# Two scores at once on the two halves of TensorE's rows, heads stacked at partitions 0 and 64, in a fused attention and expert kernel

## What is computed

```python
qkv = (x @ qkv_w.T + qkv_b).reshape(B, T, 3, H, dh)
scores = jnp.einsum('bhtd,bhsd->bhts', q, k) * scale          # dh ** -0.5
scores = jnp.where(causal, -jnp.inf, scores)
attn = jax.nn.softmax(scores, axis=-1)
seq_out = jnp.einsum('bhts,bhsd->bhtd', attn, v)
...
x = _layernorm(x + (seq_out + gated * mem_val) @ out_w.T + out_b)
x = _layernorm(x + mixture(x))   # top 2 of 8 true and 2 null experts
```

## Time and profile before

| what | value |
|---|---|
| median of 3 runs | 829.73 us (829.0 to 835.29) |
| the profiled execution's own time | 834.11 us |
| its span, first to last instruction | 832.4 us |
| mean granted TensorE clock | 0.946 |
| busy: PE, VectorE, ACT, GpSimd | 88%, 73%, 42%, 51% of the span |

### The profile page before, as it was taken

The page is one execution under the profiler, slowest core; times in us unless marked ns, Lnnn a source line. Parts: engine busy times, 40 slices in busy tenths (PEclk is TensorE's granted clock), DMA queues, the critical chain, the costliest instruction groups (busy, mean ns, idle before and its releaser), DMA issues.

```text
span 832.4 us, 12395 instructions
## 1 busy us (share of the span) xinstructions
PE 734.4 (88%) x4004; PEld 495.0 (59%) x4004; DVE 603.8 (73%) x2105; ACT 351.0 (42%) x701; POOL 422.3 (51%) x334
## 2 busy tenths in 40 slices
PE   6993998898898998999898998878899899998995
PEld 3452655565565666565565664446677676776774
DVE  2344776778878888889688877736777877787785
ACT  2211555446454545555455555842242242232410
POOL 9200894996665676668476893424134042240410
PEclk9995999999998999999899997899999999999998
DMA  7899589675564574655734747220220302303000
GB/s 274 257 234 165 127 142 144 163 115 104 130 102 84 133 119 100 152 85 138 139 69 105 139 87 170 73 101 2 77 85 18 101 10 93 102 1 102 26 24 27
DMA packets 60420, 89.88 MB, mean 108 GB/s; under 512 B 8234, under 2 KB 37316, under 8 KB 60356
## 3 DMA queue, kind: packets, MB, share of 16 engines
q1 hardware_dynamic: 60356, 89.09, 47.7%
HBM read 54.72 MB, written 33.82 MB: 106 GB/s over the span
## 4 chain that ended last, share of the span: by engine, by line
PE 47%; DVE 23%; DMA 10%; POOL 9%; ACT 4%; issue 4%; SPq 2%; ACTq 0%; POOLq 0%; DVEq 0%
PE ps L1256 15%; PE ps L374 8%; PE ps L338 7%; PE ps L327 6%; PE ps L315 6%; DVE ps L468 5%; DMA Wm<-mem_scratch 3%; DVE Ob L516 3%; DMA Q<-MT 3%; DVE A L1390 3%; ACT X L1242 2%; PE ps L1221 2%; PE ps L232 1%; POOL Pr L612 1%; DVE Z L1276 1%
## 5 line engine op out<-in xcount | busy, mean ns | idle before, releaser
L468 DVE CUSTOM_DVE_ANT_0 ps<-ps,mask 128x256 f32<-128x256 f32 (+3 forms) x512 | 236.9, 509 | 31.8 <-PE ps L315 31.0
L411 ACT ACTIVATE Pr<-ps 128x512 f32<-128x512 f32 (+2 forms) x384 | 190.1, 528 | 114.8 <-PE ps L327 110.6
L327 PE MATMUL ps<-Q,K 98*128 98x256 f32 (+2 forms) x512 | 173.2, 380 | 28.9 <-DMA Q<-MT 21.9
L315 PE MATMUL ps<-K,Q 96*128 96x256 f32 (+2 forms) x512 | 157.9, 355 | 23.2 <-DVE nmax L468 22.5
L1256 PE MATMUL ps<-ew_hi,XT 128*128 128x512 f32 x512 | 176.2, 403 | 0.0
L1390 DVE SCALAR_TENSOR_TENSOR A<-ps,cw,A 128x256 f32<-128x256 f32 x256 | 123.6, 483 | 48.5 <-PE ps L1256 36.0
L327 PEld LDWEIGHTS ps<-Q,K 98*128 98x128 f32 x512 | 94.1, 197 | 104.8 <-ACT Pr L411 61.0
L612 POOL TENSOR_SCALAR_AFFINE_SELECT Pr<-Pr 128x512 f32<-128x512 f32 x128 | 88.3, 704 | 103.2 <-ACT Pr L411 100.8
L315 PEld LDWEIGHTS ps<-K,Q 96*128 96x128 f32 x512 | 103.0, 203 | 45.8 <-DVE nmax L468 28.3
L1256 PEld LDWEIGHTS ps<-ew_hi,XT 128*128 128x128 f32 x512 | 97.0, 189 | 21.2 <-issue 0.3
L1256 PE MATMUL ps<-ew_rest,XT 128*128 128x512 f32 x256 | 101.2, 395 | 0.0
(11 more groups left out here) (190 smaller groups left out, 1049.2 us busy)
## 6 DMA issues: line engine op xcount, KB each, us to landing
qk_scratch<-HL SPq DMA_DIRECT2D x32, 512.0 KB, 3.2
Q<-qk_scratch SPq DMA_DIRECT2D x96, 128.0 KB, 4.4
K<-qk_scratch SPq DMA_DIRECT2D x96, 128.0 KB, 5.7
Pr<-xT SPq DMA_DIRECT2D x8, 512.0 KB, 7.0
xraw<-xT SPq DMA_DIRECT2D x8, 512.0 KB, 6.4
mem_scratch<-Rl SPq DMA_DIRECT2D x16, 256.0 KB, 7.5
mv_scratch<-MV SPq DMA_DIRECT2D x32, 128.0 KB, 1.8
Wm<-mem_scratch SPq DMA_DIRECT2D x16, 256.0 KB, 9.3
```

The source lines that it names most:

```text
L315: last = nc.tensor.matmul(o, Q[0:STACK, hh, P * i:P * i + P], K[0:STACK, hh, 0:n], start=True, stop=True)
L327: last = nc.tensor.matmul(o, K[0:STACK + 2, hh, P * kt:P * kt + P], Q[0:STACK + 2, hh, T - n:T], start=True, stop=True)
L411: nc.scalar.activation(probs(g % 2, kt, heads[0], len(heads)), src, ACT.Exp, scale=SCALE).then_inc(s_exp, 1)
L468: last = nc.vector.tensor_tensor_reduce(out=scores, in0=scores, in1=mask[:, T - w:T], scale=1.0, scalar=NEG, op0=ALU.add, op1=ALU.max, acc ...
```

## The change

Each head's stack is cut to its 48 used rows (`STACK = 48`), with the maxima's rows at 48 and 49, and heads with an odd number stand at partition 64 (`HALF`), so that `Q` and `K` hold two heads in each column block. `unit_parts` gives two-head units two heads of the same half: (0, 2) and (1, 3). PE issues, for each unit, the first exp score, then the first max score, and then the second ones if there are any; by the choice of LEAD = 9 (21 units ahead) the max score is always on the other half than the exp score. The transpose of the maxima, at unit `UNITS - LEAD`, so moves from unit 4 to unit 3. `HL` is held twice, and its two parts are stored by two DMAs, the high one as soon as ACT has written it. A stack is built by eight DMAs and the maxima's rows by four. Sums of columns, sizes of the maxima's inputs and the exponentials are as before. A tensor `later` keeps the addresses of what lies behind.

```diff
-LEAD = 8
+LEAD = 9
 GROUP = 4
-STACK = 96
+STACK = 48
+HALF = 64
+BROWS = 96
...
-    qk_scratch = nc.dram_tensor("qk_scratch", [NB, 4, P, 2, T], F32, kind="Internal").ap()
+    qk_scratch = nc.dram_tensor("qk_scratch", [NB, 4, 8, 2, DH, T], F32, kind="Internal").ap()
...
-        HL = sb("HL", [P, 2, T], F32R, part2)
+        HL = [sb("HL0", [P, 2, T], F32R, part2)]
...
-        Q = sb("Q", [P, H, T], F32R, part2)
-        K = sb("K", [P, H, T], F32R, part2)
+        HL.append(sb("HL1", [P, 2, T], F32R, part2))
+        later = sb("later", [P, H - 2, T], F32, part2)
+        Q = sb("Q", [P, H // 2, T], F32R, part2)
+        K = sb("K", [P, H // 2, T], F32R, part2)
...
-            return (2, [2 * (u - 8), 2 * (u - 8) + 1]) if u < 10 else (3, [2 * (u - 10), 2 * (u - 10) + 1])
+            return (2, [u - 8, u - 6]) if u < 10 else (3, [u - 10, u - 8])
+
+        def stacked(t, hh, n):
+
+            return t[HALF * (hh % 2):HALF * (hh % 2) + n, hh // 2, :]
...
+        def pe_max_waits(pe, b, g, u):
+
+            if u == 0:
+                need(pe, s_stack[g], 128, b, 128)
+            need(pe, s_max, PU, b, UNITS * g + u - 2)
+
+        def pe_max_score(pe, g, u, c):
+
+            rank, heads = unit_parts(u)
+            i, hh = QT - 1 - rank, GROUP * g + heads[c]
+            n = max(P * (i + 1), 2 * P)
+            ins = nc.tensor.matmul(S_ps[u % 3][:, c * 256:c * 256 + n], stacked(Q, hh, STACK)[:, P * i:P * i + P],
+                                   stacked(K, hh, STACK)[:, 0:n], start=True, stop=True)
+            if c == len(heads) - 1:
+                ins.then_inc(s_s, 1)
...
+        def pe_exp_waits(pe, b, g, u):
             if u == 0:
-                need(pe, s_stack[g], 96, b, 96)
...
+                need(pe, s_mrow[g], 64, b, 64)
+            need(pe, s_exp, PU, b, UNITS * g + u - 1)
...
+            ins = nc.tensor.matmul(ST_ps[u % 2][:, c * 256:c * 256 + n],
+                                   stacked(K, hh, STACK + 2)[:, P * kt:P * kt + P],
+                                   stacked(Q, hh, STACK + 2)[:, T - n:T], start=True, stop=True)
...
+        def pe_scores(pe, b, g, u, with_max):
+
+            on, ng, nu = ahead(g, u)
+            pe_exp_waits(pe, b, g, u)
+            pe_exp_score(pe, g, u, 0)
+            if with_max:
+                pe_max_waits(pe, b + on, ng, nu)
+                pe_max_score(pe, ng, nu, 0)
+            if u >= 8:
+                pe_exp_score(pe, g, u, 1)
+            if with_max and nu >= 8:
+                pe_max_score(pe, ng, nu, 1)
...
-                    pe_exp_scores(pe, b, g, u)
-                    on, ng, nu = ahead(g, u)
-                    if not (last and on):
-                        pe_max_scores(pe, b + on, ng, nu)
+                    pe_scores(pe, b, g, u, not (last and ahead(g, u)[0]))
...
-                need(act, s_scr[(j - 1) % 4 // 2], 32, b, (0, 16, 32, 16)[j])
+                need(act, s_scr[j % 2], 64, b, 32 * (j // 2))
                 m = 2 * (j % 2) + j // 2
-                nc.scalar.activation(HL[:, 0, :], J_ps[:], ACT.Identity, bias=qkb[:, m:m + 1]).then_inc(s_hi, 1)
+                nc.scalar.activation(HL[j % 2][:, 0, :], J_ps[:], ACT.Identity, bias=qkb[:, m:m + 1]).then_inc(s_hi, 1)
...
-                need(sp, s_lo, 8, b, j + 1, apart=True)
-                sp.dma_start(qk_scratch[b, j], HL[:].bitcast(F32)).then_inc(s_scr[j // 2], 16)
+                for s, done in ((0, s_hi), (1, s_lo)):
+                    need(sp, done, 8, b, j + 1, apart=True)
+                    sp.dma_start(qk_scratch[b, j, :, s], HL[j % 2][:, s].bitcast(F32)).then_inc(s_scr[j % 2], 16)
...
-            need(sp, s_scr[half], 32, b, 32, apart=True)
-            r0 = GROUP * DH * (g % 2)
-            for t, dst, parts in ((0, Q, (0, 0, 1)), (1, K, (0, 1, 0))):
-                src = qk_scratch[b, 2 * half + t][r0:r0 + GROUP * DH].rearrange("(h d) s t -> s d h t", h=GROUP)
-                for r, part in enumerate(parts):
-                    sp.dma_start(dst[DH * r:DH * r + DH, GROUP * g:GROUP * g + GROUP, :].bitcast(F32),
-                                 src[part]).then_inc(s_stack[g], 16)
+            for a in range(2):
+                need(sp, s_scr[a], 64, b, 32 * (half + 1), apart=True)
+            for t, dst, parts in ((0, Q, ((0, 2), (0, 1))), (1, K, ((0, 1), (0, 2)))):
...
+                for a in range(2):
+                    r = HALF * a
+                    for s0, n in parts:
+                        sp.dma_start(dst[r:r + n * DH, 2 * g:2 * g + 2, :].bitcast(F32),
+                                     src[a, s0 * DH:(s0 + n) * DH]).then_inc(s_stack[g], 16)
+                        r += n * DH
...
             for r in range(2):
-                sp.dma_start(Q[STACK + r:STACK + r + 1, GROUP * g:GROUP * g + GROUP, :].rearrange(
-                    "o h (i t) -> o (h i) t", i=QT).bitcast(F32), MT[:, g % 2, r, :].bitcast(F32)).then_inc(s_mrow[g], 16)
+                for a in range(2):
+                    row = HALF * a + STACK + r
+                    sp.dma_start(Q[row:row + 1, 2 * g:2 * g + 2, :].rearrange("o c (i t) -> o (c i) t", i=QT).bitcast(F32),
+                                 MT[2 * QT * a:2 * QT * a + 2 * QT, g % 2, r, :].bitcast(F32)).then_inc(s_mrow[g], 16)
...
-            for t in (Q, K):
-                nc.gpsimd.memset(t[0:STACK].bitcast(F32), 0.0).then_inc(s_cch, 1)
+            for r in (32, HALF + 32):
+                nc.gpsimd.memset(K[r:r + 32].bitcast(F32), -1.0).then_inc(s_cch, 1)
             pool.wait_ge(s_cch, 2)
-            nc.gpsimd.memset(K[STACK:STACK + 2].bitcast(F32), -1.0).then_inc(s_cst, 1)
-            pool.wait_ge(s_cst, 1)
```

More of the change, by code:

```diff
@@ L83, in build @@
         gates = sb("gates", [P, QT, NB])
-        pick = sb("pick", [STACK, P], F32R)
-        bc = sb("bc", [STACK, D], F32R)
+        pick = sb("pick", [BROWS, P], F32R)
+        bc = sb("bc", [BROWS, D], F32R)
         sc = sb("sc", [P, 16])
@@ L297, in probs, with unit_probs @@
             return Pr[:, buf, P_OFF[kt] + h0 * w:P_OFF[kt] + (h0 + nh) * w].rearrange("p (h t) -> p h t", h=nh)
+        def unit_probs(buf, kt, heads):
+            if len(heads) == 1:
+                return probs(buf, kt, heads[0], 1)
+            w = T - P * kt
+            return Pr[:, buf, P_OFF[kt]:P_OFF[kt] + GROUP * w].rearrange("p (c a t) -> p a c t", c=2, a=2)[:, heads[0]]
         def ahead(g, u):
@@ L305, in pe_max_scores @@
         def pe_max_scores(pe, b, g, u):
-            rank, heads = unit_parts(u)
-            i = QT - 1 - rank
-            n = max(P * (i + 1), 2 * P)
+            pe_max_waits(pe, b, g, u)
+            for c in range(len(unit_parts(u)[1])):
+                pe_max_score(pe, g, u, c)
+        def pe_exp_waits(pe, b, g, u):
             if u == 0:
-                need(pe, s_stack[g], 96, b, 96)
[L311 to L315, removed]
@@ L316, in pe_max_scores, with pe_exp_score @@
-            last.then_inc(s_s, 1)
-        def pe_exp_scores(pe, b, g, u):
+                need(pe, s_mrow[g], 64, b, 64)
+            need(pe, s_exp, PU, b, UNITS * g + u - 1)
+        def pe_exp_score(pe, g, u, c):
             kt, heads = unit_parts(u)
+            hh = GROUP * g + heads[c]
             n = max(T - P * kt, 2 * P)
[L321 to L329, removed]
+            ins = nc.tensor.matmul(ST_ps[u % 2][:, c * 256:c * 256 + n],
+                                   stacked(K, hh, STACK + 2)[:, P * kt:P * kt + P],
+                                   stacked(Q, hh, STACK + 2)[:, T - n:T], start=True, stop=True)
+            if c == len(heads) - 1:
+                ins.then_inc(s_st, 1)
@@ L410, in act_exp @@
             src = ST_ps[u % 2][:, 0:len(heads) * n].rearrange("p (h t) -> p h t", h=len(heads))[:, :, n - w:n]
-            nc.scalar.activation(probs(g % 2, kt, heads[0], len(heads)), src, ACT.Exp, scale=SCALE).then_inc(s_exp, 1)
+            nc.scalar.activation(unit_probs(g % 2, kt, heads), src, ACT.Exp, scale=SCALE).then_inc(s_exp, 1)
         def act_project(act, b, j):
@@ L456, in act_batch, with turned_row @@
                         last_phase["scalar"]["beside"](act, g, u)
+        def turned_row(h, i):
+            return QT * (2 * (h % 2) + h // 2) + i
         def dve_max(dve, b, g, u):
@@ L469, in dve_max @@
                     out=scores, in0=scores, in1=mask[:, T - w:T], scale=1.0,
-                    scalar=NEG, op0=ALU.add, op1=ALU.max, accum_out=nmax[:, g % 2, QT * h + i:QT * h + i + 1])
+                    scalar=NEG, op0=ALU.add, op1=ALU.max, accum_out=nmax[:, g % 2, turned_row(h, i):turned_row(h, i) + 1])
             last.then_inc(s_max, 1)
@@ L486, in dve_turned_max @@
             if g >= 2:
-                need(dve, s_mrow[g - 2], 32, b, 32)
+                need(dve, s_mrow[g - 2], 64, b, 64)
             else:
-                need(dve, s_mrow[g + 2], 32, b, 0)
+                need(dve, s_mrow[g + 2], 64, b, 0)
             nc.vector.tensor_copy(MT[:, g % 2, 0, :], M_ps[0:GROUP * QT, 0:P]).then_inc(s_mt, 1)
```

(4 more changed lines are left out.)

11 lines of the change are left out of this document (7 added, 4 removed).

## The result

The changed kernel takes 879.5 us (median of 4 executions, 867.67 to 881.97) against 829.37 us of the kernel before (4, 827.85 to 835.29): a ratio of 1.054, 95% interval 1.047 to 1.061. It is slower; 809 us, and any time inside 784 to 838, was wrong, and so was the sign. The profiled execution is the longest of the four, 881.97 us, with a mean granted clock of 0.877 (before 0.946).

What follows compares the result with a forecast made beforehand. PE (59% of the chain) and VectorE (about a third), handing over in 14.70 us groups, were taken as the bound; groups -24.4, batch 7 -1.7, rows +3, opening -1, clock +3 gave -21 us: 809 us, range 784 to 838.

Steps and rivals of the forecast that it cites:

- The clock: Attention, where PE is nearly idle: some three more stretches of half clock, +3 us in all (bounds 0 and +40).
- slower: the clock: Rival: where PE waits for VectorE or rows, 20 further low-clock stretches of 1.7 us make 840 us; chance 0.12.
- the pairs: Exp and max scores side by side, weight loads one after another: 1.6 us of PE saved a group, -0.97 on the chain.
- the breaks: Five changes of tile shape a group around transposes and projections, 0.2 us each: +1.0 us of PE, +0.60 on the chain.
- the lead: Transpose of the maxima moved from unit 4 to 3, shortening VectorE's wait: -0.55 us a group (bounds 0 and -1.4).
- the rows: The maxima's rows in four DMAs, not two, the last leaving 1.2 us later: +3 us in all (bounds -5 and +20).
- the opening: Before attention, the first stack can leave some 3 us sooner as HL is held twice: -1 us (bounds 0 and -3).
- more: Rival: the paired scores' weight loads overlap too, PE saves 2.4 us a group, 796 us; chance 0.22.
- nothing much: Rival: PE's saving turns into waits in the groups, as the other loops are close behind; 825 us, chance 0.14.
- signs for "right": Paired starts within 0.12 us, VectorE's wait for L358 under 15 us, ACT's waits for HL's stores gone, PE busy visibly less.
- sign for "wrong": 0.23 us between starts in a pair, groups still 14.7 us with longer PE waits, or a granted clock under 0.85.

Runs made afterwards that it cites:

- b_tile64: Kernel before with its zero rows taken out (stacks of 48 and 50 rows, all heads at partition 0, no two scores at once): 920.6 us against 828.23.
- a_t4r64: Changed kernel with the transpose of the maxima back at unit 4 and exp scores over 64 rows: 859.1 us, ratio 1.040 to the kernel before.
- b_t64e64: Kernel before with stacks of 48 and 50 rows at partition 0 and exp scores over 64 rows, 14 more of zeros: 895.5 us, ratio 1.079.
- a_rows64: Changed kernel with its exp scores over all 64 rows of their half, 14 more of zeros: 863.6 us, ratio 1.044 to the kernel before.
- a_turn4: Changed kernel with the transpose of the maxima back at unit 4, all else as changed: 870.4 us, ratio 1.052 to the kernel before.
- a_v32: Changed kernel with the value matmuls' weights 32 columns wide in place of 17, extra sums unused: 879.4 us, ratio 1.056 to the kernel before.
- b_lead9: Kernel before with LEAD = 9 alone (transpose at unit 3, max scores one unit earlier): 829.6 us, ratio 1.000.
- b_full: Kernel before with exp scores over 128 rows and value weights 32 columns wide: 827.9 us, ratio 0.996.

## Why the prediction was wrong

**The clock is the step that failed.** I had "+3 us (bounds 0 and +40)", and as the rival "slower: the clock" 840 us with a chance of 0.12. Place and direction were right, the trigger and the size were not: "the low stretch shown needed PE to be nearly idle". The earlier trace rows is one kind of fall; b_tile64 shows another, with PE busy for 3.25 of 3.40 us, and so does the changed kernel itself (2.99 of 3.40, and 13 of its 33 falls are like it). The change takes in 48 or 50 rows where 96 or 98 were, and packs two scores into the time of one. I had read the zero rows as work without worth, and they helped to keep the clock up.

What it costs: a line through the 28 groups of the changed kernel (length against time at 1.2 GHz) has a slope of 0.43, in the kernel before 0.79. 5.77 x 0.43 - 1.39 x 0.79 = 1.4 us of the 1.60 by which a group grew, or 39 us in 28 groups. That is an estimate, and a rough one: no group of the changed kernel was free of low clock, and its points scatter (correlation 0.61, in the kernel before 0.84). The rest, 0.2 us a group, is the line's other end, 13.82 against 13.61.

That rest is the second thing that went wrong. The span grew by 47.8 us where I had -21, and the clock makes up some 36 of these 69 us (39 where I had 3). Some 27 more lie in the 28 groups apart from the clock: I had -24.4 for the pairs, the breaks and the lead and +3 for the rows, and the lines' ends give about +6. The last 6 lie in batch 7 and the opening. So by this estimate the change would have been no gain without any low clock either; the groups of a_t4r64 that had none (12.91 against 13.69) point to a small one.

That rows move the clock and the time is shown, not only argued, by zero rows alone put in: -25 us in b_t64e64, -16 in a_rows64, -11 from a_turn4 to a_t4r64, by the medians. That the small scores lose more than the whole change does, without any two running at once, is shown by b_tile64 (+92 us). How its loss divides between rows and the smaller tile is not shown, nor what running in pairs adds to the low clock. More columns of weights (a_v32) did nothing.

The Trainium skill (TensorE: Matmul & The Clock Gate, Part 1) ties the low clock to an engine that was idle. The kernel before agrees at 227.3 us; b_tile64 at 143.5 us and the changed kernel at 288.9 us do not, and the measurement decides.

**Pairs (-1.6 us of PE, bounds 0 and 2.4).** The forecast's rests on loads one after another; they start together (303.08 and 303.08), so the mechanism was that of the rival "more". Yet such a unit takes 0.33 to 0.35 us, the 0.33 that I had for another reason, which is luck: it stands behind a wait for ACT ([0.21 <-ACT Pr L446]), and its load starts with its matmul (303.08) and not ahead of it. That this wait is the reason is my reading; no run tests it. At full clock little of it reached the group: 13.4 us in a_turn4's and a_rows64's groups without low clock, 12.9 in a_t4r64's, against 13.69. "PE's saving turns into waits" of the rival "nothing much" is what is left of it.

**Breaks (+1.0 us a group).** They exist, at my price or half of it: some 0.17 us where a score follows a transpose, and 0.09 where it follows a projection (0.211 us in the changed kernel, 0.118 in b_lead9), where I had 0.2. In the length of a group they are not seen: b_tile64 has three of the five and takes 13.52 us at full clock. That they fall into time in which PE would have waited anyway is my reading, and the 8 groups are too few to show it.

**The lead (-0.55 a group, bounds 0 and -1.4).** It was worth nothing: zero in the kernel before (b_lead9), and in the changed one between zero and +9 us (879.5 against 870.4 in a_turn4, not told apart). "elsewhere the maximum is there: nothing" was the slip: PE waited 21.3 us in 21 pieces at L396, with all of the next unit behind it.

**Rows and HL.** PE's waits for rows went from 9.4 to 14.1 us, +4.7 where I had +3. Timeline of SP, HL's store and the rows:

```profile
303.28 1.29 SPq L664 DMA_DIRECT2D qk_scratch<-HL  x2
304.62 3.50 SPq L690 DMA_DIRECT2D Q<-MT  x4
```

Four issues take 3.50 us here, where I had 4 x 0.62 from the earlier trace rows; this is a long one, since the median issue of the rows is 0.63 us and single ones take up to 1.53. The opening was put at -1 and measured +0.2.

**What would show it.** Of the signs for "right", the starts within 0.12 us and the vanished waits of VectorE and ACT were there, but PE was busy for more of the 28 groups, not less (399.56 against 377.57 us). A sign for "wrong", a granted clock under 0.85, came true (0.82).

**Open.** How much of the low clock is due to the rows, how much to the 64-row tile and how much to the pairs; what the four DMAs cost in the changed kernel (13 and 2 us by two comparisons; 3 us in the kernel before); whether paired scores can be kept beside a high clock. Neither fillers nor zero rows up to 64 did it, and no kernel here beats the one before by what can be told: b_full's interval ends at 1.000.

## What to carry to other kernels

Before you pack small matmuls side by side or trim zero padding from their rows, look at the granted clock: rows of zeros cost TensorE no time here, and taking them out, with the smaller tile that follows, cost 92 us of 828. Test such a change by its clock part alone first: only the rows cut, nothing overlapped. And a wait is moved, not removed, where the waiting engine changes; look which engine has more standing behind it.

## What the runs showed of the hardware

- The clock fell to 1.2 GHz behind 3.40 us in which PE was busy for 3.25, and stayed there for 27.3 us with PE busy for 26.76 (b_tile64, whose scores take in 48 to 50 rows); 14 more zero rows in the exp scores gave back 25 us (b_t64e64).
- More columns of the weights in the value matmuls didn't act that way: with 17 and 32, 879.5 and 879.4 us.
- Loads of 128 columns onto two halves of the rows started together (303.08), and matmuls on them within 0.01 us (303.08, 303.09).
- From a 128-row transpose to a score of 50 rows the starts were 0.20 us apart, to one of 98 rows 0.03; in a group at full clock the difference doesn't show (13.52 against 13.69 us).
